# Regular spacing for the norm tiles of the next row group in a fused MLP stage, and their subtraction ahead of the join

## The reference, cut to what matters

```python
x = x + xattn(layernorm(x), ctx)
x = x + attn(layernorm(x))
x = x + ffn(layernorm(x))
# ffn, ff_dim = 2048:
h = round8(x @ w1 + b1)            # round8: to multiples of 2**-8
h = round8(piecewise_linear_gelu(h))   # 33 break points on [-4, 4]
out = round8(h @ w2 + b2)
```

## Time and profile before

| what | value |
|---|---|
| median of 3 runs | 1573.74 us (1573.6 to 1573.89) |
| profiled execution, its own time | 1573.89 us |
| its span, first to last instruction | 1571.9 us |
| PE busy | 1557.2 us, 99% |
| DVE busy | 1226.9 us, 78% |
| ACT busy | 1035.9 us, 66% |
| POOL busy | 818.9 us, 52% |
| granted TensorE clock | 1.0 in the whole span |

### The profile page before, as it was taken

How to read it: one execution, slowest core, us unless ns; L and a number is a source line. 1 busy time by engine, 2 the same in 40 slices (tenths; PEclk the granted TensorE clock), 3 DMA queues, 4 the chain that set the end, 5 groups by cost and what they waited for, 6 DMA issues and landing times. The chain is left out here.

```text
span 1571.9 us, 30367 instructions
## 1 busy us (share of the span) xinstructions
PE 1557.2 (99%) x11066; PEld 1371.4 (87%) x11066; DVE 1226.9 (78%) x2410; ACT 1035.9 (66%) x2037; POOL 818.9 (52%) x784
## 2 busy tenths in 40 slices
PE   9999999999999999999999999999999999999998
PEld 7889899898998989989899888998898888888886
DVE  6558878888788887888788686677687788888887
ACT  3457777777777777777778542444444777868675
POOL 3318648476574765737546232143433555555554
PEclk9999999999999999999999999999999999999999
DMA  8984536446364563644534485332334831203010
GB/s 252 272 265 147 174 113 191 135 158 180 113 184 133 159 183 109 191 128 145 141 99 124 133 293 177 128 89 95 108 122 152 297 102 48 85 34 97 8 53 27
DMA packets 212051, 221.88 MB, mean 141 GB/s; under 512 B 84736, under 2 KB 156736, under 8 KB 211904
## 3 DMA queue, kind: packets, MB, share of 16 engines
q1 hardware_dynamic: 211904, 219.95, 45.5%
HBM read 158.02 MB, written 61.87 MB: 140 GB/s over the span
## 5 line engine op out<-in xcount | busy, mean ns | idle before, releaser
L79 PE MATMUL p_bank_score<-p_ctxt,p_qo 128*128 128x256 f32 x2304 | 304.5, 286 | 1.0 <-ACT p_probs L1117 0.6
L79 PEld LDWEIGHTS p_bank_score<-p_ctxt,p_qo 128*128 128x128 f32 x2304 | 288.1, 191 | 6.2 <-issue 2.4
L79 PE MATMUL p_bank_mix<-p_probt,p_ctx 128*128 128x512 f32 x1152 | 292.0, 398 | 0.5
L79 PEld LDWEIGHTS p_bank_mix<-p_probt,p_ctx 128*128 128x128 f32 x1152 | 207.4, 189 | 41.9 <-issue 3.8
L1321 DVE SCALAR_TENSOR_TENSOR p_qo<-p_bank_mix,p_odd,p_qo 128x512 fp32r<-128x512 f32 x192 | 143.8, 749 | 57.8 <-ACT p_qo L1131 50.2
L1131 ACT ACTIVATE p_qo<-p_bank_mix,p_odd 128x512 fp32r<-128x512 f32 x192 | 132.5, 690 | 68.3 <-PE p_bank_mix L79 67.7
L1117 ACT ACTIVATE p_probs<-p_bank_score,p_small 128x257 f32<-128x257 f32 x256 | 121.7, 476 | 58.6 <-DVE p_small L1302 54.1
L806 POOL TENSOR_SCALAR p_probs<-p_probs,p_small 128x256 f32<-128x256 f32 x256 | 122.1, 484 | 69.7 <-DVE p_small L1308 69.6
L800 POOL TENSOR_TENSOR p_ctx<-p_ctx_in,p_ctx 128x768 fp32r<-128x768 f32 x64 | 118.3, 1848 | 67.1 <-ACT p_ctx L1106 66.8
L795 POOL TENSOR_TENSOR p_ctx_in<-p_ctx_in,p_odd_in 128x768 f32<-128x768 f32 x64 | 118.2, 1846 | 39.7 <-DMA p_odd_in<-in_ctx_dram 39.7
L1302 DVE TENSOR_REDUCE p_small<-p_bank_score 128x1 f32<-128x257 f32 x256 | 105.6, 416 | 10.3 <-PE p_bank_score L79 7.6
(11 more groups left out here) (305 smaller groups left out, 3898.5 us busy)
## 6 DMA issues: line engine op xcount, KB each, us to landing
p_blocks_in<-in_ctx_dram SPq DMA_DIRECT2D x256, 96.0 KB, 2.4
p_ctx_in<-in_ctx_dram SPq DMA_DIRECT2D x64, 384.0 KB, 3.1
q<-p_ctx SPq DMA_DIRECT2D x64, 256.0 KB, 3.6
ffn<-p_w_raw SPq DMA_DIRECT2D x64, 256.0 KB, 2.8
p_odd_in<-in_ctx_dram SPq DMA_DIRECT2D x64, 192.0 KB, 3.6
p_x<-in_x_dram SPq DMA_DIRECT2D x32, 256.0 KB, 3.9
p_quad<-q SPq DMA_DIRECT2D x32, 256.0 KB, 3.7
p_probt<-q SPq DMA_DIRECT2D x32, 256.0 KB, 3.7
```

The costliest lines, as they stand in the source:

```text
L79: made = e.matmul(out, lhsT, rhs, start=n == 0, stop=n == last)
```

## The change

The three lists of rounds become one rule: the first tile of the next group is loaded in round 4, scaled in 5 and turned in 7, and each further tile two rounds later. So turning stays where it was (7, 9, 11, 13). Loading goes from (4, 5, 7, 9) to (4, 6, 8, 10) and scaling from (5, 6, 8, 10) to (5, 7, 9, 11). Apart from that, VectorE makes the tile's `low` ahead of `join(n - 1)` instead of behind it. This holds for the three groups that have a next one.

```diff
-        FINISHED = 5
-        LOADED, SCALED, TURNED = (4, 5, 7, 9), (5, 6, 8, 10), (7, 9, 11, 13)
-
-        def tile_at(n, rounds):
+        def tile_at(n, first):
             g, f = divmod(n, KF)
-            return [(g + 1) * NRF + rounds.index(f)] if n < NF and g + 1 < NG and f in rounds else []
+            return [(g + 1) * NRF + (f - first) // 2] if n < NF and g + 1 < NG and f >= first and (
+                f - first) % 2 == 0 and (f - first) // 2 < NRF else []
+
+        LOADED, FINISHED, SCALED, TURNED = 4, 5, 5, 7
...
-            for n in range(LOADED[0], NF + LAG):
+            for n in range(LOADED, NF + LAG):
...
                 snap(n)
-                join(n - 1)
                 for i in tile_at(n, TURNED):
                     after.norm.low(e, i, zts_next[(g + 1) % 2], i % NRF * P)
+                join(n - 1)
```

## The result

The changed kernel takes 1584.0 us (median of 5 runs, 1583.96 to 1584.48), the kernel before 1573.74 (5 runs, 1573.6 to 1573.93): 1.0065 of the time before, 95% interval 1.0052 to 1.008. That is slower by 10.3 us, above the range forecast. Its profiled execution took 1584.16 us with a span of 1582.2, also 10.3 more than the one before.

What follows compares the result with a forecast made beforehand. The prediction took PE to bound this stage by a hair; with VectorE ahead of GpSimd, 0.45 us lost around round 13 gave +0.5 in total, 1574.2 us (own range 1573.5 to 1575.6; 8 in 10 range 1573.5 to 1582.0).

Steps and rivals of the forecast that it cites:

- What bounds the kernel: Group 0: PE bounds by a hair, 10.88 us per two rounds; the loop gains 0.29 per turning pair, 0.51 per plain round.
- The scaling that moves: ScalarE, nine scalings of 1.20 us, now mostly in turning rounds: pair 10.91 us against PE's 10.88, nothing gained or lost.
- The contact with GpSimd: Turning rounds: `join`'s second operation at +1.95 or +1.96 us after `high`, GpSimd's subtraction at +1.96; whoever starts first blocks the other.
- a tie: Nine turning rounds with a scaling: VectorE's and GpSimd's starts coincide; turning point fixed only between -0.07 and +0.10 us.
- VectorE first: Main case: `join`'s second operation starts ahead of GpSimd's subtraction and lasts 0.69 us; 1574.2 us, chance 0.49 including a late DMA.
- Rival 1: GpSimd ahead of `join`'s second operation: turning round 7.14 us, 0.86 lost per pair, +7.8 in all, 1581.6; chance 0.37.
- After it plain rounds give back 0.5 us each ... so nothing more is lost: After the fourth turning round of group 0: plain rounds rebuild the lead, groups 1 and 2 have more in hand, no further loss.
- the forecast's sum: Group 0 carried forward: early pairs just met, round 13 and the hand-over to PE cost 0.45 us; total +0.5.
- Round 13: Fourth turning round, no scaling: GpSimd about 0.4 us ahead, `join`'s second operation 1.1 to 1.4, round 6.5 us, 0.2 lost to PE.
- The DMAs: Tile loads, writes and block reads between scaling and turning: some 8.5 us available against 8.1 near the worst, so covered.

Runs made afterwards that it cites:

- the kernel with the pause: Changed kernel plus one single-column ScalarE operation between `high` and `ends` in rounds that turn and scale: 1577.02 us, ratio 1.0021 to the kernel before.
- `low` alone: Kernel before with its old lists of rounds, only `low` moved ahead of `join(n - 1)`: 1580.61 us, ratio 1.0044.
- GpSimd held: Changed kernel with GpSimd's subtraction in turning rounds waiting until `join(n - 1)` is done: 1577.61 us, ratio 1.0025 to the kernel before.

## Why the prediction was wrong

**What bounds the kernel: right.** The time changed through late starts of PE, and every wait that the view prints for the changed kernel is for `low_h`.

**The scaling that moves: right where it is alone.** The new lists cost 0.0 us. But "A pair is then 10.91 us against PE's 10.88: nothing gained, nothing lost" counted only whether PE has to wait, and not that the old pair of 10.59 put 0.29 us aside each time.

**The contact with GpSimd: the step that failed, by the size of one term.** "GpSimd's subtraction starts 1.96 us after the start of `high`" came from a `high` of 0.60 us that had waited, with `ends` 0.54 behind it:

```profile
1353.77 0.73 ACT L2079 ACTIVATE p_pieces_q<-p_v,p_fixed 128x512 f32<-128x512 bf16 x1
```

Behind a scaling, `ends` starts only 0.47 to 0.49 after `high` (1271.08 to 1271.56), so the subtraction starts at +1.90 in round 7 and +1.88 in rounds 9 and 11. The second operation of `join` starts at +1.94 and +1.96, as reckoned. What was called a tie was lost by 0.05 or 0.06 us, and "I take VectorE first" was wrong in nine rounds of nine. The rule of the Trainium skill that stands in that step ("SBUF — State Buffer", section "Who interferes with whom") held in the contacts shown here, with 1.77 us for 0.69 on VectorE's side and 1.81 for 1.28 on GpSimd's.

**Rival 1 had the mechanism, and most of its size.** It said a turning round of 7.14 and 4.6 after it; measured 7.06 and 4.61. It said 1.8 us for the second operation; 1.77 and 1.78. It said +7.8 in all; up to the down of round 63 it is +7.2, with waits in all three groups as it described. The 2.5 us that it lacks of the 10.3 are less than the tail's 3.1, for which it had no term.

**"After it plain rounds give back 0.5 us each ... so nothing more is lost": wrong, in both cases.** This left the tail out, a term put at nothing without a reason. The `low_h` of down(59) ended 9.33 us ahead of it before (1542.83 against 1552.16) and 4.36 after (1554.97 against 1559.33). The tail lived on that lead: `round_up(63)` waits 2.06 us for PE before and not at all after. With the lead spent, the tail costs 3.1 us in the changed kernel, and 2.7 in the kernel with the pause, which has the pairs that the forecast assumed. Up to down(59) that kernel loses 0.45 us, just what the forecast's sum said; but its time is 1577.0 and not 1574.2. So the forecast would have been about 2.8 us short even with VectorE first. Part of that is the further contact at `join(61)`, whose second operation lasts 1.67 us there too (1556.13); in the kernels with more lead it alone was worth 0.8.

**Round 13: right in kind, short in size.** GpSimd came 0.45 us ahead of `join`'s second operation (1295.46 against 1295.91), as said, but that operation lasts 1.66 us and not 1.1 to 1.4: the row that stood for it, at 1556.61, is a subtraction of half the columns.

**The DMAs: right.** The longest landing on `z` was 3.2 us against an allowed 4.4, and the only idle time ahead of the scaling, 1.9 us, is for the statistics.

**The halves.** The prediction charged the scaling and `low` apart. The runs show 0.0 + 7.0 and together 10.3: the lists cost 3.3 us through the place of `low`, since only there does ScalarE's row get onto VectorE's. The forecast had that link in its sum, and lost it in the balance of lead.

What stays open: where between 0.03 us ahead and 0.05 us behind the order turns; what tips the granted clock behind a wait of 1.85 us; and how the tail's 3.1 us (2.7 with the pause) divide between the lead and the contact at `join(61)`.

## What to carry to other kernels

When two engines shut each other out, a forecast that ends in a tie within 0.1 us is no forecast: the two cases should share the chance and the time between them, and the cheapest experiment is to push one side by 0.1 us. Keep account of the lead of a loop and not only of waits: a change that only stops the lead from growing costs nothing until the tail, or the next disturbance, asks for it. And count a bounding engine's loss from start to start: the printed waits of 0.5 us here stood for 0.8, and three late starts that no view printed for another 0.8. Ahead of an operation that can be shut out, a wait is worse than its length, because it moves that operation onto the other engine's start.

## What the runs showed of the hardware

- Order at hundredths: with VectorE's start 0.05 or 0.06 us behind GpSimd's, VectorE's operation took 1.77 or 1.78 instead of 0.69; with 0.03 to 0.05 ahead, it kept 0.69 and GpSimd's took 1.80 or 1.81 instead of 1.28. Both held in all nine rounds of their kernels, and the two kernels are 7.0 us apart.
- The pause: a ScalarE operation of one column took 0.19 us, but put off what followed it by only 0.09 (1270.58 to 1270.67).
- Behind a scaling of 1.29 us, `ends` started 0.47 to 0.49 us after `high`; where no scaling stood ahead of `high`, 0.53 to 0.61.
- GpSimd gets in between two dependent VectorE operations 0.72 us apart: 1.66 us instead of 0.69 for the second one.
- The granted TensorE clock fell to about half for a while behind a wait of 1.85 us (`low` alone) and of 1.87 (GpSimd held), and 12 matmuls took 4.61 us instead of 3.04; behind waits of 1.84 and 1.49 us in two other kernels it stayed at 1.0.
